# The six-layer stack of a transformer kernel: both value projections and two q/k projections in one TensorE group, statistics behind the rotations

## The reference

```python
def attn_layer(x, Wqkv, qs, ksc, Wo):       # 16 heads of 64, windows of 32 tokens
    q, k, v = split heads of x @ Wqkv
    q = l2norm(q) * qs ; k = l2norm(k) * ksc
    q = q * cos * scale + rotate_half(q) * sin * scale
    k = k * cos / scale + rotate_half(k) * sin / scale
    out = local_attention(q, k, v)          # own window and the one before, softmax
    return out @ Wo
def ffn_layer(x, g, bln, W1, b1, W2, b2):
    xn = layernorm(x) * g + bln
    a, gate = split(xn @ W1 + b1)           # 341 each
    return a * gelu(gate) @ W2 + b2
for i in range(6):
    x = attn_layer(shift_tokens(x), ...) + x
    x = ffn_layer(shift_tokens(x), ...) + x
```

## Time and profile before

| | us |
|---|---|
| median of 3 runs | 4469.63 (4464.69 to 4471.03) |
| the profiled execution | 4465.72 |
| its span, first to last instruction | 4463.9 |
| PE busy | 4153.5 (93%) |
| DVE busy | 3762.2 (84%) |
| ACT busy | 3604.0 (81%) |
| POOL busy | 3147.1 (71%) |

### The profile page before, as it was taken

The page is one execution under the profiler, slowest core; times in us unless marked ns, Lnnn a source line. Parts: engine busy times, 40 slices in busy tenths (PEclk is TensorE's granted clock), DMA queues, the critical chain, the costliest instruction groups (busy, mean ns, idle before and its releaser), DMA issues. The chain is left out here.

```text
span 4463.9 us, 151456 instructions
## 1 busy us (share of the span) xinstructions
PE 4153.5 (93%) x51003; PEld 2751.8 (62%) x51005; DVE 3762.2 (84%) x9029; ACT 3604.0 (81%) x12939; POOL 3147.1 (71%) x4201
## 2 busy tenths in 40 slices
PE   6949999999999999999999999999999999677885
PEld 3426656666666666666666666666666666455543
DVE  4779989889889889889888889889889885788497
ACT  6938878888888888888888888888888887688335
POOL 2422288888888888889888888888888885444162
PEclk9969999999999999999999999999999999788886
DMA  2000000000000000000000000000000000000000
GB/s 64 0 21 1 0 8 2 2 3 17 13 2 2 2 21 8 2 3 7 17 8 2 2 12 12 8 2 3 17 12 2 2 2 2 1 0 0 30 0 20
DMA packets 38631, 37.27 MB, mean 8 GB/s; under 512 B 11382, under 2 KB 30068, under 8 KB 37748
## 3 DMA queue, kind: packets, MB, share of 16 engines
q1 hardware_dynamic: 38004, 28.97, 2.3%
HBM read 26.86 MB, written 2.10 MB: 6 GB/s over the span
## 5 line engine op out<-in xcount | busy, mean ns | idle before, releaser
L2326 ACT ACTIVATE stack_prob<-ps,stack_shift_by 128x128 f32<-128x128 f32 x3072 | 1081.2, 378 | 3.3 <-DVE stack_shift_by L2448 2.7
L2254 POOL TENSOR_TENSOR stack_qk<-stack_qk,stack_rsin 128x512 f32<-128x512 f32 x768 | 970.8, 1275 | 41.1 <-DVE stack_rsin L2473 41.0
L2261 POOL TENSOR_TENSOR stack_qk<-stack_qk,stack_inv 128x512 f32<-128x512 f32 x768 | 794.8, 1046 | 217.8 <-ACT stack_inv L2345 217.8
L2646 PE MATMUL ps<-local_wqkv,stack_xsT 128*128 128x512 f32 x1536 | 797.1, 601 | 4.5 <-DVE stack_rsin L2473 2.4
L2268 POOL TENSOR_TENSOR stack_prob<-stack_prob,stack_rs 128x512 f32<-128x512 f32 x768 | 793.0, 1044 | 1.7 <-DVE stack_rs L2455 1.7
L2326 ACT ACTIVATION_READ_ACCUMULATOR stack_prob<-ps,stack_shift_by 128x1 f32 x3072 | 671.3, 219 | 1.3 <-issue 1.3
L2448 DVE TENSOR_REDUCE stack_shift_by<-ps 128x4 f32<-128x512 f32 x768 | 524.0, 682 | 77.2 <-PE ps L2725 71.9
L2473 DVE TENSOR_TENSOR stack_rsin<-ps,stack_sin_t 128x256 f32<-128x256 f32 x1536 | 571.9, 413 | 4.7 <-issue 4.7
L2462 DVE TENSOR_TENSOR stack_qk<-ps,stack_cos_t 128x512 f32<-128x512 f32 x768 | 525.2, 684 | 37.1 <-ACT stack_sq L2334 36.1
L2480 DVE TENSOR_REDUCE stack_ss<-stack_sq 128x8 f32<-128x512 f32 x768 | 513.3, 669 | 0.7 <-ACT stack_sq L2334 0.7
L2334 ACT ACTIVATE stack_sq<-ps 128x512 f32<-128x512 f32 x768 | 468.4, 610 | 52.8 <-PE ps L2646 45.3
(11 more groups left out here) (342 smaller groups left out, 8606.0 us busy)
## 6 DMA issues: line engine op xcount, KB each, us to landing
local_wqkv<-L_ffn_Wqkv SPq DMA_DIRECT2D x30, 256.0 KB, 2.7
local_wo<-L_ffn_Wo SPq DMA_DIRECT2D x6, 512.0 KB, 4.6
out<-quantised_res SPq DMA_DIRECT2D x8, 256.0 KB, 2.3
local_w<-L_ffn_W SPq DMA_DIRECT2D x6, 341.0 KB
local_wqkv<-L_ffn_Wqkv SPq DMA_DIRECT2D x1, 1536.0 KB, 6.3
early_L_decay<-c_decay SPq DMA_DIRECT2D x1, 1024.0 KB, 10.0
local_w<-L_ffn_W SPq DMA_DIRECT2D x12, 64.0 KB
load_raw<-L_ffn_w SPq DMA_DIRECT2D x8, 64.0 KB, 1.9
```

Source lines behind the costliest of these rows:

```text
L2254: nc.gpsimd.tensor_tensor(qk[w][:, j, :, :], qk[w][:, j, :, :], rsin[j % 2][:, :, :], ALU.add).then_inc(rot_ready, 1)
L2261: nc.gpsimd.tensor_tensor(qk[w][:, j, :, :], qk[w][:, j, :, :], bcast(inv[:, w, 8 * j:8 * j + 8].unsqueeze(2), [P, 8, LH]), ALU.mult).then ...
L2326: last = nc.scalar.activation(prob[w][:, g, j, :], ps[:, 4 + g % 2, j * P:(j + 1) * P], ACT.Exp, bias=shift_by[:, w, h:h + 1], accum_out=s ...
L2646: nc.tensor.matmul(proj_bank(j), xsT[w][:, :], wqkv[:, 512 * j:512 * j + 512], start=True, stop=True).then_inc(proj_ready, 1)
```

## The change

It renames banks, changes the order of calls in all four engines' steps, and fits the waits of `project`, `project_values` and `hidden` to it. No instruction is added or taken away. The diff, cut to what matters (the waits not shown are those of `hidden`, which now uses banks 0 and 6 for chunks 0 and 2 and banks 2 and 3 for chunk 1):

```diff
-    UNIT_BANK = (1, 0, 0, 1)
+    UNIT_BANK = (0, 1, 0, 1)
-        return (ps[:, 2, :], ps[:, 3, :]) if c != 1 else (ps[:, 1, :], ps[:, 6, :])
+        return (ps[:, 2, :], ps[:, 3, :]) if c == 1 else (ps[:, 0, :], ps[:, 6, :])
@@ POOL's step
-                copy_for_values(n - 3, v, live)
+                copy_for_values(n - 2, u, live)
@@ ACT's step
+                evacuate_x(m, u, live)
+                evacuate_probs(m - 4, u, 1, 0, live)
+                evacuate_probs(m - 4, u, 1, 1, live)
                 evacuate_heads(m - 4, u, 0, live)
-                evacuate_x(m, u, live)
+                exponentials(m - 2, u, 0, live)
+                exponentials(m - 2, u, 1, live)
+                evacuate_values(m - 2, u, 1, live)
+                log_norms(m - 1, v, live)
                 evacuate_qk(m - 2, u, 1, 0, live)
-                exponentials(m - 2, u, 0, live)
                 squares(m, u, 0, live)
-                log_norms(m - 1, v, live)
                 high_half(m - 5, v, live)
                 over_norms(m - 1, v, live)
                 squares(m, u, 1, live)
-                exponentials(m - 2, u, 1, live)
...
                 else:
+                    exponentials(m - 2, u, 2, live)
+                    over_deviation(m - 6, u, live)
+                    squares(m, u, 2, live)
+                    exponentials(m - 2, u, 3, live)
                     evacuate_qk(m - 1, v, 0, 0, live)
-                    exponentials(m - 2, u, 2, live)
-                    exponentials(m - 2, u, 3, live)
                 squares(m, u, 3, live)
@@ DVE's step
                 maxima(m - 2, u, 0, live)
+                maxima(m - 2, u, 1, live)
+                bound_norms(m - 1, v, live)
                 evacuate_qk(m - 2, u, 1, 1, live)
+                evacuate_heads(m - 4, u, 1, live)
                 evacuate_values(m - 2, u, 0, live)
-                bound_norms(m - 1, v, live)
-                maxima(m - 2, u, 1, live)
                 one_over_sums(m - 3, v, 2, live)
                 one_over_sums(m - 3, v, 3, live)
+                one_over_sums(m - 2, u, 0, live)
                 cosines(m, u, 0, live)
                 sines(m, u, 0, live)
+                maxima(m - 2, u, 2, live)
+                maxima(m - 2, u, 3, live)
+                one_over_sums(m - 2, u, 1, live)
                 cosines(m, u, 1, live)
                 sines(m, u, 1, live)
                 statistics(m - 5, v, live)
...
                 else:
+                    sums_of_squares(m, u, 0, live)
                     evacuate_qk(m - 1, v, 0, 1, live)
-                    maxima(m - 2, u, 3, live)
-                    sums_of_squares(m, u, 2, live)
+                    sums_of_squares(m, u, 1, live)
                     residual(m - 4, u, layer, live)
                     norm(m - 6, u, (k - 6) % RING, live)
-                    cosines(m, u, 2, live)
-                    sines(m, u, 2, live)
+                aggregate(m - 5, v, live)
+                cosines(m, u, 2, live)
+                sines(m, u, 2, live)
+                sums_of_squares(m, u, 2, live)
                 cosines(m, u, 3, live)
@@ project: the waits of j = 0 to 3
                     if j == 0:
                         pe.wait_ge(xsT_ready, b + 1)
-                        wait(pe, rot_step, 4 * b)
...
+                        wait(pe, vals_ready[0], b - 1)
                     elif j == 1:
+                        wait(pe, vals_ready[1], b - 1)
                     elif j == 2:
+                        wait(pe, rot_step, 4 * b + 1)
                     else:
+                        wait(pe, rot_step, 4 * b + 2)
@@ project_values
+                    wait(pe, rot_step, upto(4 * b + 7 + half, 4 * TOTAL))
@@ PE's step
                 turn_qk(m - 2, u, 1, live)
+                weighted_values(m - 4, u, 1, live)
                 project_values(m - 2, u, 0, live)
+                project_values(m - 2, u, 1, live)
                 project(m, u, 0, live)
                 shift(m - 5, v, live)
                 project(m, u, 1, live)
-                weighted_values(m - 4, u, 1, live)
-                turn_probs(m - 3, v, 0, live)
-                project_values(m - 2, u, 1, live)
                 if quad:
                     turn_quad(q - 2, m, k // QUAD)
-                project(m, u, 2, live)
+                turn_probs(m - 3, v, 0, live)
                 scores(m - 2, u, 1, live)
                 if quad:
                     hidden(q - 2, m, layer)
                     output(m - 4, u, live)
-                    wait_alone(pe, env, h_ready, 3 * (q - 2) + 3)
+                    wait_alone(pe, env, h_ready, 3 * (q - 2) + 2)
                     turn_qk(m - 1, v, 0, live)
                     ffn_output(q - 2)
+                    project(m, u, 2, live)
                 else:
                     turn_qk(m - 1, v, 0, live)
+                    project(m, u, 2, live)
                     output(m - 4, u, live)
                 project(m, u, 3, live)
```

More of the change, by code:

```diff
@@ L2398, in step @@
                 squares(m, u, 1, live)
-                exponentials(m - 2, u, 1, live)
+                if quad:
+                    quad_input(q - 2, layer)
                 evacuate_probs(m - 3, v, 0, 1, live)
                 evacuate_probs(m - 3, v, 0, 0, live)
-                evacuate_values(m - 2, u, 1, live)
+                log_variance(m - 6, u, live)
                 if quad:
[L2404 to L2408, removed]
+                    over_deviation(m - 6, u, live)
                     gates(q - 2)
@@ L2412, in step @@
                     evacuate_qk(m - 1, v, 0, 0, live)
+                    squares(m, u, 2, live)
                 else:
+                    exponentials(m - 2, u, 2, live)
+                    over_deviation(m - 6, u, live)
+                    squares(m, u, 2, live)
+                    exponentials(m - 2, u, 3, live)
                     evacuate_qk(m - 1, v, 0, 0, live)
-                    exponentials(m - 2, u, 2, live)
-                    exponentials(m - 2, u, 3, live)
                 squares(m, u, 3, live)
-                evacuate_probs(m - 3, v, 1, 0, live)
-                evacuate_probs(m - 3, v, 1, 1, live)
             layered_loop(act, NB, step)
@@ L2633, in project @@
                             wait(pe, rot_step, 4 * b - 1)
[L2634 to L2640, removed]
+                    elif j == 1:
                         wait(pe, vals_ready[1], b - 1)
                         if isinstance(b, int):
-                            wait(pe, rot_step, 4 * b + 1)
                             wait(pe, rot_step, 4 * b)
+                    elif j == 2:
+                        wait(pe, rot_step, 4 * b + 1)
+                    else:
+                        wait(pe, rot_step, 4 * b + 2)
                     new_layer(b, wq_loaded[j])
@@ L2651, in project_values @@
                     pe.wait_ge(xvT_ready, b + 1)
[L2652 to L2661, removed]
+                    wait(pe, rot_step, upto(4 * b + 7 + half, 4 * TOTAL))
+                    if isinstance(b, int):
+                        wait(pe, vals_ready[half], b)
                     new_layer(b, wv_loaded[half])
@@ L2817, in hidden @@
                         pe.wait_ge(ffn_loaded, FFN_LOADS * (layer_of(q, layer) + 1))
+                        pe.wait_ge(rot_step, upto(4 * m + 1, 4 * TOTAL))
+                        if isinstance(q, int):
+                            pe.wait_ge(vals_ready[0], upto(m - 1, TOTAL))
+                        pe.wait_ge(oT_ready[1], upto(m - 3, TOTAL))
+                        pe.wait_ge(xT_ready, q + 1)
+                    elif c == 1:
                         pe.wait_ge(probT_ready[0][0], upto(m - 2, TOTAL))
                         pe.wait_ge(probT_ready[0][1], upto(m - 2, TOTAL))
[L2820 to L2823, removed]
                     else:
```

## The result

The changed kernel takes 4778.57 us (median of 6, 4775.59 to 4781.12) against 4469.56 in the same runs: 1.0691 times as long, 95% interval 1.068 to 1.0702, 309 us more. The prediction was 4715, range 4650 to 4810: the direction was right and the two stops came where they were forecast; the size was 64 us short of the 309.

What follows compares the result with a forecast made beforehand. PE bounds the kernel before; after the change DVE's order was to set the step. 3 x 15.95 + 23.5 = 71.35 us per four steps against 66.25, times 48: +245 us, 4715 us, range 4650 to 4810.

Steps and rivals of the forecast that it cites:

- the two stops: On DVE in each plain step: idle 1.7 us before the first cosine and 0.7 before the third maximum.
- PE is the bound before: Kernel before, plain step: PE busy all 14.37 us and never waiting, DVE and POOL within half a microsecond.
- Grouping saves 0.20 us a step: On PE: one pair of mode changes goes, 0.10 us each side; 38 us less if PE stayed the bound.
- The shared bank stops P0, and DVE with it: P0 waits for the value copy in bank 0; DVE stands still 1.7 us before the first cosine.
- The maxima behind sines(0): On DVE: maxima(2) and (3), now directly behind sines(0), wait for scores(1), another 0.7 us of idle.
- The period by DVE's order, 15.95: Plain step: 4.58 us from value copy to maxima(2) plus 11.37 of other DVE work, 15.95 us against 14.37.
- the step on the moved statistics: squares(2) on ACT waits for the first sum; chain to the next first maximum has 0.2 us slack, taken as zero.
- The rival that named it, 4789: ACT's late chain takes over: plain steps 16.3, quad 24.0, +319 us, 4789; chance 11%.
- My theory of one ring: Plain step bound by one chain through all engines, from value copy via P0, scores(1), squares(2) to next value copy: 16.30 us.
- that of two: Two rings: through squares(2), exponentials(3) and q/k copy, 16.31 us; through over_norms, POOL's seven operations and turn_probs(1), 16.15.

Runs made afterwards that it cites:

- squares(2) experiment: The changed kernel with ACT's squares(2) of a plain step moved behind exponentials(3) and the q/k copy: 4753.1 us, ratio 1.0631.
- maxima_late: The changed kernel with maxima(2), maxima(3) and one reciprocal moved behind cosines(1) and sines(1) on DVE: 4751.5 us, ratio 1.0622.

## Why the prediction was right, and where it was short

*PE is the bound before.* Shown: one more wait on PE lengthens each plain step of the kernel before by its full 1.12 us.

*Grouping saves 0.20 us a step.* Right on PE's own work, 14.2 us; it did not reach the time, not even with the old banks, where the new order brought waits of its own (plain step 14.90).

*The shared bank stops P0, and DVE with it.* Right in mechanism and place: the stop before the first cosine is 1.78 us (1.7 forecast), and the wait alone, put into the old kernel, costs 5.1%, where the whole change costs 6.9. The moved weighted values alone cost 3.5%. The two are not terms of a sum, since in the change PV1 fills most of P0's wait and P0's rotation no longer has to precede PV1.

*The maxima behind sines(0).* The stop is there, 0.61 + 0.08 as forecast. As a term of the sum it was right only while DVE's round is what binds; taking it out gave back 0.20 us, not 0.69, for the two reasons above.

*The period by DVE's order, 15.95.* This is the term that was mis-sized: 16.31 was measured, three times a group of four, 3 x 0.36 = 1.1 of the 1.28 us by which the group was missed (the quad step's 23.7 for 23.5 is the rest), 48 x 1.28 = 61 of the 64 us. DVE itself needed less than I gave it: 16.31 less its idle of 1.78, 0.61, 0.12 and 0.11 and 0.08 for each stop is 13.37, not 13.58 (0.14 of it is the norm, 0.49 us before and 0.35 after), so its round would have taken 15.9. What failed is the step on the moved statistics: "I take zero; the other end is +0.4 us a step". I measured that chain's slack at the wrong place, the first maximum. It goes on: behind scores(0) PE has turn_qk(1), 0.64 like turn_probs, and weighted_values(1), 1.02, and from PV0 to the next value copy it is 1.16. On my own figures that is 10.56 + 0.65 + 1.02 + 0.95 + 0.64 + 1.02 + 1.16 = 16.0, already more than the 15.95 of DVE's order: there was no slack. The measured chain reached turn_probs(1) at v + 10.87 where I had 10.56: ACT's copy ended 0.12 later than I had it, and PE started 0.25 behind its end and not 0.06. From there 4.28 + 1.16 make the 16.31. The squares(2) experiment shows that this chain binds: without its wait the step is 16.15. That the forecast missed by no more than 0.36 us a step is in part luck: the chain that it summed and the chain that bound are of nearly one length. The rival that named it, 4789, came closer than the forecast.

*After that.* My theory of one ring fell, then that of two. In the changed order at least three chains of nearly one length go round the step: through squares(2) (16.31), through the second rotation and POOL (16.15), through output and residual (16.0 to 16.1). A fourth place is P1, behind ACT's copy of PV1. Shown is that after opening one the wait stands at the next, each with its row; that these are all, or that 15.9 is the floor of this grouping, is not. The second chain's whole length was not tried on its own.

## What to carry to other kernels

When two products come to share a PSUM bank, price the whole detour, product, copy, product, next reader, at the first engine that is nearly full, and test it by adding the bare wait to the old kernel: here one wait cost 225 us while the grouping could save 38 at most. In a software pipeline with four engines at 82 to 90% of a step, a stop's length is not what its removal returns; follow each chain once round the step, back to where it started, and treat a slack of 0.2 us as none. Before moving a product next to another of its kind, write down what its old place covered.

## What the runs showed that I had not expected

A DVE instruction that nobody touched, the norm, takes between 0.34 and 0.75 us by what POOL is doing when it starts; in maxima_late that ate 0.40 of the 0.69 us that the edit should have returned. And filling a stop of 1.78 us with 1.2 us of work returned nothing that can be told apart (1.0672 against 1.0691).

The hand-over from ACT's q/k copy to PE's transposes took 0.25 us from the copy's recorded end (2626.72 + 0.62 to 2627.59), where DVE to PE took 0.06.
